# Layer 0's two attentions: the cross-attention's steps placed ahead of the self-attention's on TensorE, ScalarE and VectorE

## The reference

```python
x = x + _L0_xattn_ref(_layernorm(x), ctx_1024, 32, ...)   # cross-attention, one head, only the 32 largest scores kept
x = x + _L0_attn_ref(_layernorm(x), ...)                  # self-attention, 16 heads of 8, rotary positions
x = x + _L0_ffn_ref(_layernorm(x), ...)                   # router and 8 experts
```

## Time and profile before

| | |
|---|---|
| median of 3 runs | 1725.52 us (1721.81 to 1727.04) |
| profiled execution, own time | 1724.12 us |
| its span | 1722.3 us |
| layer 0's attentions | from the start to 377.4 us of the span |
| PE, DVE, ACT, POOL busy over the span | 87%, 63%, 50%, 31% |

### The profile page before, as it was taken

One profiled execution on the slowest core, in us unless ns is written; L12 is line 12 of the kernel. 1 busy time (PEld: TensorE's weight loads), 2 busy tenths in 40 slices (PEclk: granted clock), 3 DMA queues, 4 the chain that ended last, 5 costly groups with the idle time before them and its releaser, 6 DMA issues. The chain is left out here.

```text
span 1722.3 us, 46099 instructions
## 1 busy us (share of the span) xinstructions
PE 1506.3 (87%) x15538; PEld 1145.9 (67%) x15538; DVE 1078.3 (63%) x3391; ACT 853.4 (50%) x2372; POOL 531.7 (31%) x1145
## 2 busy tenths in 40 slices
PE   3887888857889699999999999789999999599998
PEld 2666666646567566666666666567777777488887
DVE  3888888846310267777777777656666666333333
ACT  2555555521233267777777777534444444144443
POOL 1444444420714334444444444422222222000000
PEclk9999999975889889999999999999999999699999
DMA  5455633200111211111111111000000000000000
GB/s 186 162 168 168 228 117 104 81 1 0 51 38 49 76 35 34 34 34 34 33 33 33 33 33 34 13 1 0 0 0 0 0 0 1 1 7 12 6 12 12
DMA packets 67039, 80.26 MB, mean 47 GB/s; under 512 B 8422, under 2 KB 54643, under 8 KB 66864
## 3 DMA queue, kind: packets, MB, share of 16 engines
q1 hardware_dynamic: 64848, 76.06, 14.7%
q0 software_dynamic: 2144, 3.60, 0.7%
HBM read 69.52 MB, written 10.91 MB: 47 GB/s over the span
## 5 line engine op out<-in xcount | busy, mean ns | idle before, releaser
L1621 ACT ACTIVATE c_pr<-c_pS,c_nm 128x257 f32<-128x257 f32 x512 | 238.2, 471 | 97.5 <-DVE c_nm L1755 97.5
L1755 DVE TENSOR_REDUCE c_nm<-c_pS 128x1 f32<-128x257 f32 (+1 forms) x384 | 173.2, 505 | 42.7 <-PE c_pS L1501 42.4
L1995 ACT ACTIVATE s_k<-s_pK 128x512 f32<-128x512 f32 x128 | 76.4, 597 | 177.3 <-PE s_pK L1922 177.3
L1505 PE MATMUL c_pT<-cst,c_pr 128*128 128x128 f32 x1024 | 163.2, 284 | 0.0
L1375 ACT ACTIVATE f_hid<-f_pH,vec 128x512 f32<-128x512 f32 x128 | 88.0, 687 | 128.5 <-PE f_pH L1337 127.2
L1397 DVE SCALAR_TENSOR_TENSOR X<-f_pY,f_mk,X 128x128 f32 x256 | 72.1, 344 | 111.6 <-PE f_pY L1347 111.6
L1922 PEld LDWEIGHTS s_pK<-s_hT,AH 128*128 128x128 f32 x1024 | 124.0, 195 | 25.9 <-ACT s_k L1995 22.8
L1922 PE MATMUL s_pK<-s_hT,AH 128*128 128x128 f32 x1024 | 137.7, 284 | 0.5 <-ACT s_hT L1990 0.5
L1505 PEld LDWEIGHTS c_pT<-cst,c_pr 128*128 128x128 f32 x1024 | 111.4, 141 | 37.7 <-issue 37.7
L1347 PEld LDWEIGHTS f_pY<-f_w,f_hid 128*128 128x128 f32 x1024 | 122.3, 192 | 5.1
L1347 PE MATMUL f_pY<-f_w,f_hid 128*128 128x128 f32 x1024 | 124.1, 276 | 0.0
(11 more groups left out here) (300 smaller groups left out, 3188.5 us busy)
## 6 DMA issues: line engine op xcount, KB each, us to landing
a_ctxT<-in_ctxT SPq DMA_DIRECT2D x32, 514.0 KB, 3.7
c_ctxT<-in_ctxT SPq DMA_DIRECT2D x128, 128.5 KB, 2.2
a_ctxN<-in_ctxR SPq DMA_DIRECT2D x32, 512.0 KB, 4.1
f_w<-in_f_w SPq DMA_DIRECT2D x16, 256.0 KB, 3.3
rows_in<-a_zero SPq DMA_DIRECT2D x7, 322.5 KB, 4.3
f_h<-rows_in SPq DMA_DIRECT2D x7, 322.5 KB
a_ctxL<-in_ctxL SPq DMA_DIRECT2D x128, 16.0 KB, 3.5
f_w<-in_f_w SPq DMA_DIRECT2D x16, 128.0 KB, 3.3
```

Of the source, the lines that this page charges most:

```text
L1505: mm = pe.transpose(pT[:, c, j, :], pr[:, b % 2, j, c * P:(c + 1) * P], k("ident"))
L1621: act.activation(pr[:, b % 2, c, :], pS[:, c, 0:S], ACT.Exp, bias=nm[:, c:c + 1], accum_out=den[:, b % 2, c:c + 1]).then_inc(e_ready.sem, 1)
L1755: dve.tensor_reduce(nm[:, c:end], pS[:, c:end, 0:S], AX.X, ALU.max, negate=True).then_inc(max_ready.sem, 1)
```

## The change

In the `slot` of TensorE, ScalarE and VectorE of `attend_layer0` the steps of group `u` (cross-attention) move ahead of the neighbouring steps of `z` and `a` (self-attention). No instruction is added, removed or changed in size; buffers, waits and transfers are as before. GpSimd's and SyncE's programs are untouched.

```diff
 # TensorE
                 run(turn_a, a)
+                run(turn_weights, u)
                 run(turn_self_weights, z)
-                run(turn_weights, u)
+                run(lambda u: sums(u, p, r), u)
                 run(self_queries_keys, a)
-                run(lambda u: sums(u, p, r), u)
+                run(turn_sums, u)
                 run(self_sums, z)
-                run(turn_sums, u)
+                run(sums_by_values, u)
                 run(self_values, a)
                 run(turn_self_sums, z)
-                run(sums_by_values, u)
                 run(queries, x)
+                run(project, u)
                 run(self_project, z)
-                run(project, u)
                 run(queries_by_keys, x)
 # ScalarE
                 run(turned_sums, u)
+                run(sums_by_values, u)
                 run(turned_self_sums, z)
-                run(sums_by_values, u)
                 run(queries, x)
 # VectorE
                 run(lambda g: n1.vector_rows(dve, x_of(g)), w_)
+                run(lambda u: sums_with_last(u, p, r), u)
                 run(mark(1), t)
-                run(lambda u: sums_with_last(u, p, r), u)
                 run(rotate, a)
                 run(self_inverse_sums, z)
...
                 run(scale_w, w_)
+                run(add_output, u)
                 run(add_self_output, z)
+                run(rows_u, u)
                 run(rows_z, z)
-                run(add_output, u)
                 run(negated_max, t)
                 run(lambda g: n3.vector_moments(dve, g), z)
-                run(rows_u, u)
                 run(mark(3), t)
```

## The result

| | before | after |
|---|---|---|
| median | 1723.66 us (4 runs, 1720.84 to 1727.04) | 1740.32 us (4 runs, 1737.83 to 1747.05) |
| ratio to before | | 1.0102, 95% interval 1.0067 to 1.0137 |
| span of the profiled execution | 1722.3 us | 1745.3 us |
| end of layer 0's attentions (first VectorE instruction of the routing) | 378.62 us | 402.28 us |

The change makes the kernel slower by 1.0%: 16.7 us by the medians, 17.6 by the ratio. The forecast was +3.8 us with a range that ends at 1736.5, so the measured time lies outside. All of the difference lies where the change is: the attentions end 23.7 us later in the profiled execution, and the whole span is 23.0 us longer.

The account below looks back on a forecast made before the run. It took VectorE's list (7.13 us) plus a ScalarE-TensorE chain (3.14) to set each slot. +0.20 times 26 = +5.2, + 0.1 - 1.1 - 0.4 = +3.8, giving 1729.3 us, range 1718 to 1736.5.

Parts of the forecast that it names:

- `sums_with_last` no longer waits: VectorE, each loop slot: the idle 0.27 ahead of sums_with_last goes and it starts 0.76 earlier.
- `self_inverse_sums` waits for `self_sums` behind `turn_sums`: VectorE, each loop slot: a chain of 2.10 us leaves it idle 0.83 and starts self_inverse_sums 0.47 later.
- The tail gives 0.27 back: From scale_w to negated_max: the wait for self_project goes, 1.16 against 1.43 us, 0.27 saved per slot.
- The circle runs from `keep_logits` over VectorE's list to `negated_max`: Loop slot: VectorE works through its list for 7.13 us, then a ScalarE and TensorE chain of 3.14 closes it.
- rival A: At self_inverse_sums: new wait shorter than what it replaces; without any wait 0.63 saved per slot, 1707.7 us; chance 0.15.
- +0.20 per slot: Each of 26 loop slots: +0.47 at self_inverse_sums less 0.27 in the tail, +5.2 us in all.
- D: the clock: Rival, TensorE in the loop: a few more slots with slowed matmuls, 0.57 us each, 1733 us; chance 0.05.
- Slot 3 and the ends, -1.5: Outside the regular loop: slot 3 -1.1 through shorter VectorE waits, slots 31 to 33 some -0.1, -0.1 and -0.2.

Follow-up runs that it names:

- e2: Kernel before with only the change's tail (project ahead of self_project, add_output and rows_u first); ratio 1.0105, +18 us, full-clock slot 10.63.
- e4: Kernel before with one more VectorE copy of 128x128 behind keep_logits; ratio 0.9999, 0 us, full-clock slot 10.27.
- e1: The change with self_sums back ahead of turn_sums and sums_by_values back behind self_values; ratio 1.0045, +8 us, full-clock slot 10.46.
- e8: Kernel before reordered: both sums ahead of L440, self_sums ahead of turn_sums, VectorE's order to match; ratio 0.9952, -8 us, full-clock slot 9.73.
- e6: The change with 13 throw-away transposes per slot in four idle places of TensorE; ratio 1.0028, +5 us, no slow slots.
- e5: Kernel before with one more VectorE add of 128x192 ahead of negated_max; ratio 1.0098, +17 us, full-clock slot 10.47.
- e3: The change with four throw-away transposes per slot ahead of self_scores; ratio 1.0068, +12 us, three slow slots.
- e9: e8 with nine throw-away transposes per slot in TensorE's idle places; ratio 0.9912, -15 us, no slow slots.
- e10: Kernel before with ten throw-away transposes per slot in TensorE's idle places; ratio 1.0013, +2 us, full-clock slot 10.27.
- e7: The change with its tail undone (self_project and add_self_output first again); ratio 1.0089, +15 us, full-clock slot 10.69.

## Why the prediction was wrong

- *`sums_with_last` no longer waits.* Right: it starts 1.96 behind `keep_logits`, forecast 2.01.
- *`self_inverse_sums` waits for `self_sums` behind `turn_sums`.* Right, and close: 4.05 behind `keep_logits`, forecast 4.11. The idle shown is 0.58 and not 0.83 for two reasons: `rotate` starts 0.12 later than forecast (2.80, where 2.68 was forecast), because L440, now behind `sums`, ends only then and takes 1.16 rather than 1.06; and the profile counts idle from the end of `rotate` (0.69 long), while the forecast counted from its start plus 0.61.
- *The tail gives 0.27 back.* Right in the changed kernel (`scale_w` to `negated_max` 1.16, as forecast), and wrong as a thing by itself: e2.
- *The circle runs from `keep_logits` over VectorE's list to `negated_max`.* Wrong for its first part. e4 shows slack there, e1 that TensorE's groups set `self_inverse_sums`. It didn't hurt the sum, since in the changed kernel `sums_with_last` has nothing to wait for and the chain behind it was counted right. But rival A's price (0.63 a slot saved if `self_inverse_sums` doesn't wait) could not be had in this order: e1, where that wait is down to 0.16, is 0.19 a slot slower than before. Only e8, with both sums ahead of L440, saves 0.54.
- *+0.20 per slot.* Measured +0.28. `negated_max` moves by 0.23: 0.42 at `self_inverse_sums`, 0.09 from there to `scale_w`, less 0.28 in the tail; and 0.05 come behind it, where `turn_z` waits 0.29 for VectorE's `scale_z` (0.22 before). With 26 x 0.28 = 7.3 and the 1.4 taken off for the ends the forecast would have been +6, inside the range.
- *"D: the clock", at 0.05 and +0.57 in a few slots.* This is the step that failed. The sum took the loop at full clock in all 26 slots because the kernel before has it. In the changed kernel ten slots lose some part of it, each 1.0 to 2.2 us, 14.1 in the profiled execution; e6 puts it at some 13 of 18 over all runs. The mechanism was named, but its price was 0.57 in each of a few slots; measured is more than double that, in ten.
- *Slot 3 and the ends, -1.5.* Wrong too: slot 3 takes 13.0 against 10.69 in the profiled executions, with matmuls still at half speed where they are full before (`self_values` 1.94 against 1.08). The wait ahead of `sums_with_last` does fall, from 1.54 to 0.94, but `rotate` waits 1.15 for L440 and `add_output` 1.82 for `project`, where 0.81 was to go. In e2, whose front is that of before, it takes 11.5, in e1 11.5, in e4 12.5. It varies by over 1 us from kernel to kernel, so how much of it is the change's stays open.

Shown is that the order of before, made 0.20 a slot longer, loses the clock as the change does (e5), that one kernel takes 8 us less in the runs that keep more of the clock (e8), and that filling TensorE's idle pieces brings it back without shortening a slot (e3, e6, e9), while it saves nothing where the clock was lost in one slot only (e10). So the order of the change is not needed for the loss. Open is what makes 10.27 us safe: 9.73 (e8), 10.46 (e1), 10.47 (e5), 10.55 (the change), 10.63 (e2) and 10.69 (e7) all lose clock, at distances of some 20 us in e8, 45 to 65 in e2 and e7 and 85 to 95 in e1, e3 and the change, so it isn't that longer slots lose more. Nor is it the longest idle piece of TensorE: between 60 and 320 us that is 0.85 in e2, 0.81 in e5 and 0.67 in the change, but 0.53 in e7, as in the kernel before, and 0.40 in e8. That the distances are regular suggests that it depends on how the slot's idle pieces fall against something that repeats by itself; that is only argued.

## What to carry to other kernels

Before a step is moved ahead in an engine's order, ask what then stands behind it and whether that was free to start: `turn_sums` came forward by 0.8 us and took the ready `self_sums` with it into a wait. That a loop holds its full granted clock says nothing of the next variant of it: here 0.2 us more in a slot of 10.27 cost the clock (e5), 12 us beside the 5 of the length itself, and an order may look bad or good for that reason alone. Look at the granted clock of each variant, and try throw-away transposes in TensorE's idle pieces before two orders are compared.

## What the runs showed of the hardware that I had not expected

- TensorE loses half its clock in a loop where it never stands still for a full microsecond. The Trainium skill ("TensorE: Matmul & The Clock Gate", section "A second HAM failure mode: psum-queue depth-cycling") tells of a bf16 kernel in which TensorE's brief idling between groups of matmuls makes its clock swing between the two levels. The trace agrees with the swing: 1.00 and 0.54 to 0.57 by turns in the windows above (a window that is mostly at the lower level), with no idle piece over 0.67 us in the loop ahead of the first fall. That the idling is behind it fits e3, e6 and e9; what tips it stays open.
- The same loop with one VectorE instruction more (0.27 us at `negated_max`, none on TensorE) went from 1 to 5 slots with half-clock stretches, which began at 135, 145, 159, 224 and 309 us.
- A stretch at half clock lasted some 3.4 us in the loop, or twice that and no longer, worked out from the mean clock of windows around it (0.57 over 4.0 us, 0.54 over 7.5 us).
- Nine to thirteen fp32 transposes of 128x128 per slot, some 0.12 us each from start to start (five of them span 0.74 and one is 0.27 long), lengthened a full-clock slot by 0.05 us at most and brought the granted clock of 60 to 320 us from 0.93 to 1.00 in the changed kernel and from 0.94 to 1.00 in the new order.
